# A graph layer with gather and scatter: attributes four groups ahead, clears and first gathers unpaced, single split buffers, 29 groups gathered ahead

## The reference, cut to what matters

```python
def ssp(x): return softplus(x) - log(2)
# x: (50000, 256); src, dst: (50000,), dst sorted, src random; edge_attr: (50000, 64)
h = x @ W_in2f                                   # 256 x 256
Wij = (ssp(edge_attr @ Wf1 + bf1) @ Wf2 + bf2) * edge_weight
m = segment_sum(h[dst] * Wij, src)               # added up by row src
m = ssp(m @ Wo1 + bo1) @ Wo2 + bo2
out = layernorm(x + (x + m))                     # by row of 256
```

## Time and profile before

| | |
|---|---|
| median of 3 runs | 1875.04 us (1873.83 to 1876.91) |
| the profiled execution | 1860.02 us, its span 1858.3 us |
| busy in the span | PE 1747.4 us (94%), DVE 1506.0 (81%), ACT 1482.4 (80%), POOL 1428.4 (77%) |
| DMA | 363.45 MB, mean 196 GB/s |
| granted TensorE clock | 0.975 of full speed on average |
| first scatter starts | 221.51 us |
| phase two's first load | 1402.13 us |

### The profile page before, as it was taken

How to read it: one execution, slowest core, us unless ns; L and a number is a source line. 1 busy time by engine, 2 the same in 40 slices (tenths; PEclk the granted TensorE clock), 3 DMA queues, 4 the chain that set the end, 5 groups by cost and what they waited for, 6 DMA issues and landing times. The chain is left out here.

```text
span 1858.3 us, 36496 instructions
## 1 busy us (share of the span) xinstructions
PE 1747.4 (94%) x11376; PEld 1546.2 (83%) x11376; DVE 1506.0 (81%) x3750; ACT 1482.4 (80%) x2945; POOL 1428.4 (77%) x1385
## 2 busy tenths in 40 slices
PE   4689899999999999999999999989886999999995
PEld 3577788888888888888888888878776999999995
DVE  3567688888888888888888888876675999999996
ACT  3566688888887878787878787866666999999996
POOL 6542378878878878878878878778664999999997
PEclk9889999999999999999999999999997999999998
DMA  9999857666666666666666566677665899999994
GB/s 320 330 339 336 273 109 127 115 123 116 122 114 125 115 120 122 118 123 117 122 112 124 112 125 114 126 145 143 138 105 170 323 362 363 360 361 361 361 361 172
DMA packets 177339, 363.45 MB, mean 196 GB/s; under 512 B 25622, under 2 KB 76264, under 8 KB 177148
## 3 DMA queue, kind: packets, MB, share of 16 engines
q1 hardware_dynamic: 101128, 257.75, 40.7%
q0 software_dynamic: 75136, 102.45, 32.6%
q10 hardware_dynamic: 884, 0.92, 0.2%
HBM read 206.90 MB, written 154.12 MB: 194 GB/s over the span
## 5 line engine op out<-in xcount | busy, mean ns | idle before, releaser
L358 POOL DMA_INDIRECT acc<-sums,src_ix x392 | 633.2, 1615 | 171.4 <-issue 120.9
L344 POOL DMA_INDIRECT xg<-in_x,dst_t x392 | 392.2, 1000 | 200.7 <-issue 107.6
L389 POOL TENSOR_SCALAR sums<-sums,neg_mean,rstd 128x256 f32<-128x256 f32 x392 | 283.4, 735 | 10.2
L625 ACT ACTIVATE m_h<-pair,wgt_t 128x256 fp32r<-128x256 f32 x392 | 164.2, 475 | 113.3 <-PE pair L413 113.3
L499 PE MATMUL pair<-m_h,same 128*128 128x256 f32 (+1 forms) x980 | 248.0, 288 | 1.2 <-DVE m_l L786 1.2
L499 PE MATMUL pair<-m_l,same 128*128 128x256 f32 (+1 forms) x980 | 242.2, 282 | 0.0
L413 PE MATMUL pair<-wo_h,msg_h 128*128 128x256 f32 (+1 forms) x784 | 234.5, 299 | 4.0 <-DVE m_l L786 1.9
L769 DVE SCALAR_TENSOR_TENSOR pair<-pair,bias_w,h_sb 128x512 f32<-128x512 f32 x196 | 147.8, 754 | 108.2 <-PE pair L413 108.1
L413 PE MATMUL pair<-wo_l,msg_h 128*128 128x256 f32 (+1 forms) x784 | 223.1, 285 | 0.0
L413 PE MATMUL pair<-wo_h,msg_l 128*128 128x256 f32 (+1 forms) x784 | 222.1, 283 | 0.0
L531 PE MATMUL pair<-w_in_h,ssp_l 128*128 128x256 f32 (+1 forms) x784 | 220.2, 281 | 0.0
(11 more groups left out here) (96 smaller groups left out, 5394.3 us busy)
## 6 DMA issues: line engine op xcount, KB each, us to landing
acc<-fill SPq DMA_DIRECT2D x197, 256.0 KB, 3.8
xg<-in_x SPq DMA_DIRECT2D x97, 512.0 KB, 6.1
sums<-acc SPq DMA_DIRECT2D x97, 512.0 KB, 6.7
out<-sums SPq DMA_DIRECT2D x97, 512.0 KB, 4.7
attr<-in_edge_attr SPq DMA_DIRECT2D x196, 128.0 KB
srcb<-in_src_rows SPq DMA_DIRECT2D x98, 256.0 KB
xg<-in_x,dst_t POOLq DMA_INDIRECT x392, 3.7
acc<-sums,src_ix POOLq DMA_INDIRECT x392
```

What stands on the lines that cost most here:

```text
L344: pool.indirect_dma_start(xg[0:g.p, g.xs, r], None, t["x"], bass.IndirectOffsetOnAxis(ap=dst_t[0:g.p, r, g.n:g.n + 1], axis=0)).then_inc(x ...
L358: pool.indirect_dma_start(acc, bass.IndirectOffsetOnAxis(ap=src_ix[g.slot][0:g.p, r:r + 1], axis=0), sums[0:g.p, g.slot, r], None, compute ...
L389: last = pool.tensor_scalar(normed[0:g.p, g.n % NRING, r], res[0:g.p, u, r], neg_mean[0:g.p, u, r:r + 1], rstd[0:g.p, u, r:r + 1], ALU.add ...
L625: act.activation(m_h[0:g.p, r], bank[6][0:g.p, k * D:(k + 1) * D], ACT.Copy, scale=col(wgt_t, r, g)).then_inc(mh_sb, 1)
```

## The change

The attributes' ring has four groups (`ARING` = 4), and the loop of SP's queue is written anew: in turn n it loads the attributes of n + 4, the source rows of n, 15 clears and, from n = 82, a group of x. The limit of four clears in flight is gone: all count on one semaphore. The ring of gathered rows has 16 groups, 29 groups are gathered ahead, and the gathers of the head no longer wait for the landing of those before; a group's four gathers count on one semaphore. 276 gathers are then spread over the 94 groups. The ring of results has 14. To make room, the split parts of x and ssp and the 0/1 matrices have one buffer each, so that a write waits for the product of the group before; in phase two, `ssp2` takes x's and ssp's parts as its two buffers. Some small tiles move into larger ones.

```diff
-RING = 13
-XRING = 12
-ARING = 2
+RING = 14
+XRING = 16
+ARING = 4
 SRING = 2
-AHEAD = 24
+AHEAD = 29
 FIRST_CLEARS = 36
-IN_FLIGHT = 4
-CLEARS_A_STEP = 16
+CLEARS_A_STEP = 15
...
-        x_h, x_l = (sb(n, [P, 2, H, R, P], F32R) for n in ("x_h", "x_l"))
+        x_h, x_l = (sb(n, [P, H, R, P], F32R) for n in ("x_h", "x_l"))
...
-        ssp_h, ssp_l = (sb(n, [P, 2, H, R, P], F32R) for n in ("ssp_h", "ssp_l"))
+        ssp_h, ssp_l = (sb(n, [P, H, R, P], F32R) for n in ("ssp_h", "ssp_l"))
...
-        same = sb("same", [P, 2, R * (R + 1) // 2, P], F32R)
+        same = sb("same", [P, R * (R + 1) // 2, P], F32R)
...
-        ssp2_h, ssp2_l = ([b[:, k] for k in range(2)] for b in (ssp_h, ssp_l))
+        ssp2_h, ssp2_l = [ssp_h, x_h], [ssp_l, x_l]
...
-            load_attr(1)
+            for n in range(1, ARING):
+                load_attr(n)
             load_src(0)
...
-                    wait(sp, cleared[c % IN_FLIGHT], c // IN_FLIGHT * 16)
                     sp.dma_start(acc[a:b, :].rearrange("(p k) d -> p (k d)", k=CLEAR),
-                                 fill[0:(b - a) // CLEAR].rearrange("p k d -> p (k d)")).then_inc(cleared[c % IN_FLIGHT], 16)
+                                 fill[0:(b - a) // CLEAR].rearrange("p k d -> p (k d)")).then_inc(cleared, 16)
...
-            for n in range(2, G + 1):
-                if n < G:
-                    load_attr(n)
-                load_src(n - 1)
-                clear_to(FIRST_CLEARS + (n - 1) * CLEARS_A_STEP)
-                if G - XRING <= n - 2:
-                    fetch_x(group((n - 2) % XRING))
+            for n in range(G):
+                if n + ARING < G:
+                    load_attr(n + ARING)
+                if n:
+                    load_src(n)
+                clear_to(FIRST_CLEARS + (n + 1) * CLEARS_A_STEP)
+                if G - XRING <= n:
+                    fetch_x(group(n % XRING))
...
-            for n in range(G - 1, G):
-                fetch_x(group(n % XRING))
...
-                    if r % 2 == 0 and 0 < g.n < AHEAD:
-                        b = group(g.n - 1)
-                        pool.wait_ge(xg_in[b.xs][r // 2], xg_count(b))
...
-                            for u in range(IN_FLIGHT):
-                                pool.wait_ge(cleared[u], 16 * len(range(u, CLEARS, IN_FLIGHT)))
+                            pool.wait_ge(cleared, 16 * CLEARS)
...
-                    pe.wait_ge(xg_in[g.xs][q], xg_count(g))
+                    pe.wait_ge(xg_in[g.xs], xg_count(g))
...
-                    wait(act, h_ps, (g.n - 1) * H)
+                    wait(act, h_ps, g.n * H)
...
-                    wait(act, w_ps, (g.n - 1) * H)
+                    wait(act, w_ps, g.n * H)
...
-                        wait(dve, y_ps, (g.n - 1) * 2)
+                        wait(dve, y_ps, g.n * 2)
...
-                    wait(dve, h_ps, (g.n - 1) * H)
+                    wait(dve, h_ps, g.n * H)
...
-                    wait(dve, w_ps, (g.n - 1) * H)
+                    wait(dve, w_ps, g.n * H)
```

More of the change, by code:

```diff
@@ L173, in build @@
         ssp2 = [sums[:, MRING + DEPTH + NRING + k].rearrange("p r d -> p (r d)").rearrange("p (h n) -> p h n", h=H) for k in range(2)]
-        ssp2_h, ssp2_l = ([b[:, k] for k in range(2)] for b in (ssp_h, ssp_l))
+        ssp2_h, ssp2_l = [ssp_h, x_h], [ssp_l, x_l]
         wo2 = attr[:, G % ARING].rearrange("p (h d) -> p h d", h=H)
         squares = srcb[:].rearrange("p u c -> p (u c)").bitcast(F32).rearrange("p (r d) -> p r d", d=D)
-        total, neg_mean, square, veps, rstd = (sb(n, [P, DEPTH, R]) for n in ("total", "neg_mean", "square", "veps", "rstd"))
+        total, neg_mean, square, veps, rstd = (
+            to_spare[:, 0, k * DEPTH * R:(k + 1) * DEPTH * R].rearrange("p (d r) -> p d r", r=R) for k in range(5))
         dve_own = sem("dve_own")
@@ L182, in build @@
         bo1_in, fill_made = sem("bo1_in"), sem("fill_made")
-        cleared = [sem(f"cleared{u}") for u in range(IN_FLIGHT)]
+        cleared = sem("cleared")
         made = sem("made")
@@ L192, in build @@
         srcb_in = [sem(f"srcb_in{u}") for u in range(SRING)]
-        xg_in = [[sem(f"xg_in{u}_{q}") for q in range(2)] for u in range(XRING)]
+        xg_in = [sem(f"xg_in{u}") for u in range(XRING)]
         added = sem("added")
@@ L235, in xg_count @@
         def xg_count(g):
-            return sum(16 * R // 2 for n in range(g.xs, g.n + 1, XRING))
+            return sum(16 * R for n in range(g.xs, g.n + 1, XRING))
         def col(table, r, g):
@@ L453, in stage @@
                     transposed(m, bank[4][:].rearrange("f (r e) -> f r e", r=R)[:, :, 0:g.p], w_in_h, w_in_l,
-                               [x_h[:, g.par, k, :, 0:g.p] for k in range(H)], [x_l[:, g.par, k, :, 0:g.p] for k in range(H)]).then_inc(h_ps, 1)
+                               [x_h[:, k, :, 0:g.p] for k in range(H)], [x_l[:, k, :, 0:g.p] for k in range(H)]).then_inc(h_ps, 1)
                 return stage
@@ L466, in stage @@
                     transposed(m, bank[5][:].rearrange("f (r e) -> f r e", r=R)[:, :, 0:g.p], wf2_h, wf2_l,
-                               [ssp_h[:, g.par, k, :, 0:g.p] for k in range(H)], [ssp_l[:, g.par, k, :, 0:g.p] for k in range(H)]).then_inc(w_ps, 1)
+                               [ssp_h[:, k, :, 0:g.p] for k in range(H)], [ssp_l[:, k, :, 0:g.p] for k in range(H)]).then_inc(w_ps, 1)
                 return stage
@@ L498, in stage @@
                             for m in (m_h, m_l):
-                                last = pe.matmul(o, same[0:g.p, g.par, FROM[a] + b - a, 0:g.p], m[0:g.p, a],
+                                last = pe.matmul(o, same[0:g.p, FROM[a] + b - a, 0:g.p], m[0:g.p, a],
                                                  start=a == 0 and m is m_h, stop=a == b and m is m_l)
@@ L542, in _ @@
                 act.dma_start(wf1[k * A:(k + 1) * A, :], t["L0_gnn_Wf1"]).then_inc(wf1_in, 16)
-            for b, name in ((bf1, "L0_gnn_bf1"), (bf2, "L0_gnn_bf2")):
-                act.dma_start(b[:], t[name]).then_inc(b_in, 16)
+            for b, name in ((bf1[:], "L0_gnn_bf1"), (bf2, "L0_gnn_bf2")):
+                act.dma_start(b, t[name]).then_inc(b_in, 16)
             for w, name, got in ((w_in, "L0_gnn_W_in2f", w_in_in), (wf2, "L0_gnn_Wf2", wf2_in), (wo1, "L0_gnn_Wo1", wo1_in)):
@@ L563, in stage @@
                     act.wait_ge(xt_ps, g.n * 2 + q + 1)
-                    wait(act, h_ps, (g.n - 1) * H)
-                    high(x_h[:, g.par, :, 2 * q:2 * q + 2, 0:g.p], bank[q][:].rearrange("f (h k e) -> f h k e", h=H, k=2)[:, :, :, 0:g.p], xh_sb)
+                    wait(act, h_ps, g.n * H)
+                    high(x_h[:, :, 2 * q:2 * q + 2, 0:g.p], bank[q][:].rearrange("f (h k e) -> f h k e", h=H, k=2)[:, :, :, 0:g.p], xh_sb)
                 return stage
@@ L598, in stage @@
                     act.wait_ge(ssp_sb, g.n * H + h + 1)
-                    wait(act, w_ps, (g.n - 1) * H)
-                    high(ssp_h[:, g.par, h], bank[2 + h][:].rearrange("m (r e) -> m r e", r=R), ssph_sb)
+                    wait(act, w_ps, g.n * H)
+                    high(ssp_h[:, h], bank[2 + h][:].rearrange("m (r e) -> m r e", r=R), ssph_sb)
                 return stage
@@ L655, in ssp2_high @@
                 wait(act, o_ps, (g.n - 1) * 2)
-                act.activation(ssp2_h[g.par].rearrange("m h r e -> m (h r e)"), ssp2[g.par][:].rearrange("m h n -> m (h n)"), ACT.Copy).then_inc(ssp2h_sb, 1)
+                act.activation(ssp2_h[g.par][:].rearrange("m h r e -> m (h r e)"), ssp2[g.par][:].rearrange("m h n -> m (h n)"), ACT.Copy).then_inc(ssp2h_sb, 1)
             def deviation(g):
@@ L747, in stage @@
                         dve.wait_ge(srcb_in[g.n % SRING], (g.n // SRING + 1) * 16)
-                        wait(dve, y_ps, (g.n - 1) * 2)
+                        wait(dve, y_ps, g.n * 2)
                     sources = srcb[0:g.p, g.n % SRING].rearrange("x (r e) -> x r e", r=R)[:, :, 0:g.p]
-                    dve.scalar_tensor_tensor(out=same[0:g.p, g.par, FROM[a]:FROM[a] + R - a, 0:g.p], in0=sources[:, a:R],
+                    dve.scalar_tensor_tensor(out=same[0:g.p, FROM[a]:FROM[a] + R - a, 0:g.p], in0=sources[:, a:R],
                                              scalar=col(src_t, a, g), in1=later[0:g.p, 0:R - a, 0:g.p], op0=ALU.is_equal, op1=ALU.mult,
```

26 lines of the change are left out of this document (13 added, 13 removed).

## The result

The changed kernel took **1887.43 us**, median of 4 runs (1885.14 to 1891.06), against 1875.45 for the kernel before (1873.83 to 1876.91, 4 runs): ratio 1.0066, 95% interval 1.0047 to 1.0085. It is slower by 0.7%. The forecast was 1857.0, range 1843 to 1871. The profiled execution took 1891.06 us with a span of 1889.3. That of the kernel before, 1860.02 us, isn't one of its four runs here, which were all 13.8 us or more slower.

The account below looks back on a forecast made before the run. POOL's chain (clears, then 94 groups) was taken to decide the first phase. Phase two starting at 1384.1 instead of 1402.1 gave -18.0 us, other terms 0: 1875.04 - 18.0 = 1857.0 us, range 1843 to 1871.

Parts of the forecast that it names:

- T0 = 227: End of the clears and start of POOL's first scatter, forecast at 227 us, 5.5 us later than before.
- 2.5 us earlier, at 228.4: End of the head: PE's turn of group 13 was to come at 228.4 us, 2.5 us earlier.
- Gathers not paced: Head: POOL drops 26 waits of 33.9 us but then waits for the clears anyway; costed at nothing.
- the flood costs rate: Rival, head: unlimited clears beside gathers lower the transfer rate; 10% lower gives first scatter at 256, 1886 us; chance 0.12.
- The engines have nothing left to give: Head: at 337 GB/s and a DMA share of 0.96, attributes are late because many bytes stand ahead.
- the DMA engines go faster: Rival, head: with its queue always filled it reaches phase two's 361 GB/s, giving 1844 us; chance 0.16.
- Attributes four ahead: Head: the stall on attributes goes, source rows are next late, and PE enters the middle 2.5 us earlier.
- POOL's period 11.85: First phase: POOL's time per scattered group falls from 11.99 to 11.85 us, midway to 11.73, through fewer gathers.
- POOL is no faster: Rival, first phase: POOL's time per group stays 11.99 us, gaining 5 us, for 1870 us; chance 0.14.
- Last turn and tail: End of first phase: group 97 turned at 1342.9 us, then 41.25 us to phase two at 1384.1.
- PE idles: End of first phase before the change: PE waits for gathers 33.1 us in 13 places; to fall to some 10.
- Single split buffers: First phase: one buffer instead of two costs 0 to 0.1 us a group where PE isn't the bound; taken as 0.

Follow-up runs that it names:

- b_unpaced: The kernel before with only the pacing of the head's gathers taken out, clears still four in flight: 1859.34 us, ratio 0.9985.
- b_nolimit: The kernel before with only the limit of four clears in flight taken out, gathers still paced: 1838.57 us, ratio 0.9874.
- b_both: The kernel before with both the limit on clears and the pacing of gathers taken out, nothing else: 1835.73 us, ratio 0.9861.
- a_again: The changed kernel, unaltered, run again on chip B, one of the study's four chips: 1816.80 us, ratio 0.9765 to the kernel before.
- a_attr2: The changed kernel with attributes loaded two groups ahead instead of four: 1815.10 us, ratio 0.9777 to the kernel before.
- a_src3: The changed kernel with attributes three groups ahead instead of four and source rows three instead of two: 1812.30 us, ratio 0.9768 to the kernel before.
- a_ahead24: The changed kernel with 24 groups gathered ahead instead of 29: 1823.79 us, ratio 0.9819 to the kernel before.
- a_third: The changed kernel, unaltered, run on chip C: 1815.51 us, ratio 0.9778 to the kernel before.
- a_tail12: The changed kernel with the gathers behind the scatters spread over the first 86 scatters instead of 94: 1834.39 us, ratio 0.9878 to the kernel before.

## Why the prediction was wrong, by its own steps

It was wrong in sign in the first measurement and on chip D, and wrong in size on chips B and C (on A the changed kernel wasn't run), by two different steps.

**The head, in the first measurement: T0 = 227, and PE entering the middle "2.5 us earlier, at 228.4".** These are the terms that failed. They measured 250.2 and 258.5, because of the hole: the sum has no term for engines that take up finished work late. On chip B the same kernel has 200.6 and 203.1, so some 50 us of T0 are the hole's. The place in the prediction where such a term belonged is "Gathers not paced … I cost this at nothing", with the lifted limit beside it. Alone both are harmless: b_unpaced gives 0.9985 (0.9959 to 1.0010), and b_nolimit is faster. But the cover that I named, the wait for the clears, covers POOL only, while pacing and the limit were also what kept POOL and SP from issuing without a pause. In two sets of runs (the first and chip D) kernels without both stand still in the head, and the changed one turns group 2 67 us later than on chip B (107.5 against 40.3). Nothing in the trace of before shows that: it has both pauses. That the missing pauses are what lets the hole come is argued, not shown: on chip B b_both has neither and no hole, and on chip D no kernel with one of them was run.

The rival "the flood costs rate" came nearest in its number, T0 = 256 and 1886 against 250.2 and 1887, and it was partly luck. From 18 to 45 us the rate is as high as on chip B, over 400 GB/s. From 45 to 95 it is lower, with SP's 15 clears taking 20 to 21 us instead of 12 to 14; whether requests compete there isn't shown. From 98 to 110 nobody asks for bytes.

**T0 = 227, on chips B and C.** This is the term that was mis-sized there: T0 is 200.6 in a_again, 26 us earlier. The bytes were right: 382 GB/s for 200 us are 76.4 MB, against the 76.0 worked out. The rate was wrong, by the sentence "The engines have nothing left to give" and the ceiling of 0.99 taken from another stretch. A share of 0.96 is no measure of the rate that is left: with four clears in flight the head moves 337 GB/s, with 16 or without limit 381 and 382. The rival "the DMA engines go faster" had the mechanism at 0.16 and gave 1844; its rate of 361 was too low. The 358 GB/s of the Trainium skill (DMA: Bandwidth & Descriptors, Where 436 GB/s comes from), which I set beside it, is no bound here, and neither is phase two's rate: the measurement decides.

**Attributes four ahead.** Right in kind: the attributes' stall went and the source rows came in its place (22.3 us). That the deeper ring is worth nothing by itself, a_attr2 shows; that the source rows were next, a_src3.

**POOL's period 11.85, between 11.73 and 11.99.** Measured over 80 groups 11.59 to 11.63, outside both ends. Five groups more ahead give 0.24 (a_ahead24 against a_third), nearly all of the 0.26 expected; where the rest comes from is open. The pause for the previous group's additions, for which I took half of it back, got shorter over these groups, not longer: the gap ahead of a group's first scatter averages 0.35 us where it was 0.49. Then it grows to some 2 us from group 80 on, with the additions that land late while SP loads x (a_tail12): groups 80 to 93 take 13.39 us each. So the product in the sum, 93 x 11.85 = 1102, came out at 1100.9, by two errors that cancel. The prediction had also carried the 11.99 of the first 80 groups on to group 93, where the kernel before takes 12.68 from there: by its own numbers (221.5 + 93 x 11.99 + 15.0) that kernel's last turn would be at 1351.6, and it is at 1360.9. Some 9 of the 18 us forecast came from this slip, and the 5 us that the case "POOL is no faster" gains with T0 later and the period unchanged are the same slip.

**Last turn and tail.** Forecast 1342.9, measured 1317.2, 25.7 us earlier: T0 gives 26.4 and the product 1.1, and the way from scatter 93 to the turn takes 1.8 back. The 33.1 us for which "PE idles" for gathers count weight loads and products together, and much of that time twice: 15.7 us are PE's products, in 6 places. In a_again the same count in the same window falls to 9.2, as expected (some 10):

```profile
  DMA xg<-in_x,dst_t: 9.2, 6
```

(The 19.7 us in four places of a_tail12's expectation are of the whole span: 15.4 of them stand ahead of the program's first turn.)

The tail is 41.0 us, as taken, but isn't fixed (a_tail12).

**Single split buffers, the rest, phase two.** At 0, 0 and 456.2: right. PE repeats every (1272.0 - 203.1) / 81 = 13.20 us on chip B; phase two takes 456.9.

The sum on chip B: phase two starts at 1358.2 instead of 1402.1, 43.9 us earlier, of which T0 is 20.9 and POOL's chain behind it, with the tail, 23.1. Forecast were 18.0, with T0 5.5 us later and the chain and tail 23.5 shorter: the chain's gain came out as forecast by the cancelling above, and T0 had the wrong sign. In the first measurement T0 is 28.7 us later than before, the chain behind it 1.4 us longer since PE's steps in the middle are late too, and phase two starts 30.1 later. That it came out 12 us slower by the medians, and not 30, is because the kernel before also took 15.4 us more there than in its profiled execution, and the changed one 3.6 less than in its own.

## What to carry to other kernels

A DMA share near one says that the engines are occupied, not that the bytes can't come faster: what is in flight decides, and a limit of four transfers of 256 KB cost 12% of the rate here. When two producers of transfers lose their pauses in the same change, the pauses themselves may have been doing something, which these runs suggest and don't show; run the change on more than one chip before believing a gain or a loss of 1%, and run the changed kernel itself beside its variants. Ask of every transfer moved forward in a queue what in that queue it pushes back, and whether the time is won back later: the last gathers came in time, and the last scatters came 20 us late.

## What the runs showed that I had not expected

- One kernel gave 0.9765 to 0.9790 on two chips and 1.0078 on a third, with before's own time differing by less than 0.5%: 1857.2 to 1860.6 and 1865.5 us.
- On chip D DVE stood 62.7 us ahead of an instruction whose last input had been written 26.8 us before it started, with some two thirds of the records of semaphore updates left in the trace.
- While SP loads x for phase two, the additions of POOL's scatters land 5 us behind the last scatter instead of 2 to 4, and POOL's period goes to 13.2 us even with no gathers left to issue.
- The head moved 382 GB/s over 200 us with the shares summing to 1.03, in slices 402 and 404 GB/s, above the 361 of phase two.
- 16 clears in flight are as good as any number: 1817.0 and 1816.8 us.
